# Attention scores of a fused fp32 block: two pairs of PSUM banks regrouped as three single banks, and a fourth bank for the row maxima

## What is computed

```python
q = (x @ wq).reshape(b, s, 32, 32)
k = (x @ wk).reshape(b, s, 8, 32);  v = (x @ wv).reshape(b, s, 8, 32)
k = jnp.repeat(k, 4, axis=2);       v = jnp.repeat(v, 4, axis=2)
scores = einsum('bihd,bjhd->bhij', q, k) * 32 ** -0.5
scores = where(causal, scores, finfo.min)
out = einsum('bhij,bjhd->bihd', softmax(scores), v).reshape(b, s, 1024)
x = layernorm(x + out @ wo)
```

## Time and profile before

| | us |
|---|---|
| median of 3 runs | 3541.24 |
| lowest, highest | 3540.5, 3547.18 |
| the profiled execution's own time | 3546.64 |
| its span, first to last instruction | 3544.9 |
| attention, in that span | 552.0 to 2607.6 |
| from one middle group's first exponential to the next one's | 125.5 |

### The profile page before, as it was taken

The page is one execution under the profiler, slowest core; times in us unless marked ns, Lnnn a source line. Parts: engine busy times, 40 slices in busy tenths (PEclk is TensorE's granted clock), DMA queues, the critical chain, the costliest instruction groups (busy, mean ns, idle before and its releaser), DMA issues. The chain is left out here.

```text
span 3544.9 us, 62208 instructions
## 1 busy us (share of the span) xinstructions
PE 3439.6 (97%) x25458; PEld 2429.2 (69%) x25458; DVE 1978.4 (56%) x3577; ACT 1468.0 (41%) x1839; POOL 1738.5 (49%) x747
## 2 busy tenths in 40 slices
PE   8999998999999999999999999999959999999999
PEld 7888885566666666666666666666538888888887
DVE  3122116777667677776767767776425666642222
ACT  3111112555555555555555555555532222221111
POOL 0000002888988898898889889889420000000000
PEclk9999997999999999999999999999979999999999
DMA  6344325121111111112111111210037778755553
GB/s 214 113 125 118 113 90 120 30 53 50 33 43 49 46 29 51 49 32 52 51 37 38 51 48 31 53 32 8 12 117 212 233 230 224 205 197 177 178 172 128
DMA packets 248221, 340.63 MB, mean 96 GB/s; under 512 B 55440, under 2 KB 150288, under 8 KB 247952
## 3 DMA queue, kind: packets, MB, share of 16 engines
q1 hardware_dynamic: 247952, 336.87, 32.3%
HBM read 203.08 MB, written 133.17 MB: 95 GB/s over the span
## 5 line engine op out<-in xcount | busy, mean ns | idle before, releaser
L683 DVE TENSOR_REDUCE p_part_max<-p_qm 128x1 f32<-128x512 f32 (+3 forms) x2240 | 1408.3, 671 | 578.3 <-PE p_qm L533 328.7
L503 POOL TENSOR_TENSOR p_psums<-p_psums,p_probs 128x1024 f32<-128x1024 f32 x620 | 1475.4, 2380 | 93.4 <-ACT p_probs L642 2.8
L646 ACT ACTIVATE p_probs<-p_km 128x1024 f32<-128x1024 f32 x896 | 878.8, 1021 | 480.7 <-PE p_km L561 411.1
L533 PE MATMUL p_qm<-p_k_st,p_q_st 96*128 96x512 f32 (+3 forms) x2560 | 913.5, 421 | 12.5 <-DMA p_q_st<-q_hi 10.8
L533 PEld LDWEIGHTS p_qm<-p_k_st,p_q_st 96*128 96x128 f32 x2560 | 481.1, 194 | 254.7 <-issue 113.0
L561 PE MATMUL p_km<-p_q_st,p_k_st 97*128 97x512 f32 x1792 | 599.5, 416 | 13.6 <-ACT p_probs L646 7.8
L568 PE MATMUL p_o<-p_probs,p_v 128*32 128x256 f32 (+1 forms) x9216 | 564.8, 371 | 0.0
L568 PEld LDWEIGHTS p_o<-p_probs,p_v 128*32 128x32 f32 x9216 | 270.7, 110 | 216.7 <-issue 45.1
L561 PEld LDWEIGHTS p_km<-p_q_st,p_k_st 97*128 97x128 f32 x1792 | 311.6, 191 | 112.9 <-ACT p_probs L646 73.5
L499 POOL TENSOR_TENSOR p_psums<-p_probs 128x1024 f32<-128x1024 f32 x110 | 261.7, 2379 | 222.1 <-ACT p_probs L646 222.1
L32 POOL MEMSET p_ident<- 128x128 f32 x2 | 0.4, 204 | 556.3 <-POOLq L63 543.5
(11 more groups left out here) (150 smaller groups left out, 4101.3 us busy)
## 6 DMA issues: line engine op xcount, KB each, us to landing
p_q_st<-q_hi SPq DMA_DIRECT2D x128, 256.0 KB, 4.7
p_x_raw<-in_xT SPq DMA_DIRECT2D x64, 256.0 KB, 3.5
q_hi<-p_out_hi SPq DMA_DIRECT2D x64, 256.0 KB, 2.0
q_lo<-p_out_lo SPq DMA_DIRECT2D x64, 256.0 KB, 2.3
p_q_st<-q_lo SPq DMA_DIRECT2D x64, 256.0 KB, 4.5
attended_T<-p_o_raw SPq DMA_DIRECT2D x128, 128.0 KB
p_a_raw<-attended_T SPq DMA_DIRECT2D x32, 512.0 KB, 4.8
p_recip<-reciprocals SPq DMA_DIRECT2D x128, 128.0 KB, 6.7
```

Source lines behind the costliest of these rows:

```text
L503: pool.tensor_tensor(sums[:, :, :], sums[:, :, :], probs[(n * NS + s) % PB][:, :, :], ALU.add).then_inc(added, 1)
L533: last = pe.matmul(bank[:, x * keys:(x + 1) * keys], q_st[par][0:ROWS, c, h + x, sub * P:(sub + 1) * P], k_st[par][0:ROWS, j * CK:j * CK + ...
L646: act.activation(tile[:, :, :].rearrange("p h q -> p (h q)"), km[s % 2][:, :, :].rearrange("p a b -> p (a b)"), ACT.Exp, scale=SCALE).then ...
L683: dve.reduce_max(part_max[c][:, h:h + heads, sub, j], qm[bank_of(i)][:, 0:item_width(i)].rearrange("p (h k) -> p h k", h=heads), AX.X).the ...
```

## The change

`QM` is 4. The scores have `KM` = 3 single banks instead of two pairs. A step is handled as a list of halves, `HALVES`: [0, 1] off the diagonal, [1, 0] in the first diagonal step, [1] in the second. Halves are counted through all groups, 136 in each. Each half is one bank, one count of `scored`, one activation of 512 elements and one count of `exp_done`; PE makes half u after exponential u - 3. Matmuls and their order are the same, and the banks in use stay 8: 4 + 3 + 1. All waits on `exp_done` and `scored` elsewhere are rewritten to the same points in counts of halves.

```diff
-    QM = 3
+    QM = 4
+    KM = 3
+    HALVES = [[1] if t == 2 * c + 1 else [1, 0] if t == 2 * c else [0, 1] for c, t in STEPS]
+    HALVES_BEFORE = [sum(map(len, HALVES[:s])) for s in range(NS + 1)]
+
+    def halves(n, s):
+
+        return n * HALVES_BEFORE[NS] + HALVES_BEFORE[s]
...
-        km = [ps(f"p2_km{i}", [P, 2, BANK]) for i in range(2)]
+        km = [ps(f"p2_km{i}", [P, BANK]) for i in range(KM)]
...
-                        sp.wait_ge(scored, n * NS + FIRST_STEP[2 * c + 2])
+                        sp.wait_ge(scored, halves(n, FIRST_STEP[2 * c + 2]))
...
-                        pool.wait_ge(exp_done, n * NS + s + 1)
+                        pool.wait_ge(exp_done, halves(n, s + 1))
...
             def scores(n, par, s):
                 c, t = STEPS[s]
-                at_least(pe, exp_done, n * NS + s - 1)
...
+                for i, x in enumerate(HALVES[s]):
+                    u = halves(n, s) + i
+                    at_least(pe, exp_done, u - KM + 1)
+                    if t >= 2 * c:
+                        four = km[u % KM][:, :].rearrange("p (h q) -> p h q", h=REP)
+                        masked = x == t - 2 * c
                         last = pe.matmul(four, keys, q_st[par][0:ROWS + 1, c // 2, :, q0 + x * P:q0 + (x + 1) * P],
-                                         start=True, stop=x > first)
...
+                                         start=True, stop=not masked)
+                        if masked:
+                            last = pe.matmul(four, ident_bf[:, :], mask_k[:, :].unsqueeze(1).to_broadcast([P, REP, P]),
+                                             start=False, stop=True)
+                    else:
+                        two = km[u % KM][:, :].rearrange("p (h q) -> p h q", h=2)
                         last = pe.matmul(two, keys, q_st[par][0:ROWS + 1, c // 2, 2 * x:2 * x + 2, q0:q0 + CQ],
                                          start=True, stop=True)
-                last.then_inc(scored, 1)
+                    last.then_inc(scored, 1)
...
-                pe.wait_ge(exp_done, n * NS + steps[-1] + 1)
+                pe.wait_ge(exp_done, halves(n, steps[-1] + 1))
...
-                act.wait_ge(scored, n * NS + s + 1)
...
+                for i, x in enumerate(HALVES[s]):
+                    u = halves(n, s) + i
+                    act.wait_ge(scored, u + 1)
+                    if t >= 2 * c:
+                        act.activation(tile[:, :, x * P:(x + 1) * P], km[u % KM][:, :].rearrange("p (h q) -> p h q", h=REP),
+                                       ACT.Exp, scale=SCALE).then_inc(exp_done, 1)
+                    else:
+                        act.activation(tile[:, 2 * x:2 * x + 2, :].rearrange("p h q -> p (h q)"), km[u % KM][:, :],
+                                       ACT.Exp, scale=SCALE).then_inc(exp_done, 1)
```

More of the change, by code:

```diff
@@ L439, in group @@
                     if what == "load q":
-                        sp.wait_ge(scored, n * NS + FIRST_STEP[2 * c + 2])
+                        sp.wait_ge(scored, halves(n, FIRST_STEP[2 * c + 2]))
                         load_q(b2, g2, par, c)
                     elif what == "load k":
-                        sp.wait_ge(scored, n * NS + FIRST_STEP[NC - 1] + SUB * (c + 1))
+                        sp.wait_ge(scored, halves(n, FIRST_STEP[NC - 1] + SUB * (c + 1)))
                         load_k(b2, g2, par, c)
@@ L545, in scores @@
                 c, t = STEPS[s]
-                at_least(pe, exp_done, n * NS + s - 1)
                 if t == 0 and c % 2 == 0:
                     pe.wait_ge(m_in[par][c // 2], q_loads(n, par) // 3)
[L549 to L553, removed]
-                        last = pe.matmul(four, keys, q_st[par][0:ROWS + 1, c // 2, :, q0 + x * P:q0 + (x + 1) * P],
-                                         start=True, stop=x > first)
[L556 to L560, removed]
+                keys, q0 = k_st[par][0:ROWS + 1, t * P:(t + 1) * P], (c % 2) * CQ
+                for i, x in enumerate(HALVES[s]):
[4 more added lines that the diff above has]
+                        masked = x == t - 2 * c
+                        last = pe.matmul(four, keys, q_st[par][0:ROWS + 1, c // 2, :, q0 + x * P:q0 + (x + 1) * P],
+                                         start=True, stop=not masked)
[4 more added lines that the diff above has]
+                        two = km[u % KM][:, :].rearrange("p (h q) -> p h q", h=2)
                         last = pe.matmul(two, keys, q_st[par][0:ROWS + 1, c // 2, 2 * x:2 * x + 2, q0:q0 + CQ],
                                          start=True, stop=True)
-                last.then_inc(scored, 1)
+                    last.then_inc(scored, 1)
             def weighted(lhs, rhs, at, o, first):
```

## The result

The changed kernel takes 3568.8 us (median of 4 runs, 3565.0 to 3572.8) against 3544.1 before, a ratio of 1.007 with a 95% interval of 1.0054 to 1.0085. Timed again beside other kernels it gave 3567.3 against 3543.7, 1.0071 (1.0051 to 1.009). So it is slower by 24 to 25 us where 15 were forecast. The measured 3568.8 lies inside the stated range, 3532 to 3584, and 12 us over its likeliest value, 3557.

The account below looks back on a forecast made before the run. The prediction took PE's stream plus PE's waits as the bound. Middle groups +20 us, opening -7.4 and closing +2.8 summed to +15 us, 3557 us against the median of the runs, range 3532 to 3584.

Parts of the forecast that it names:

- What bounds: Attention's middle groups: no other engine is full, so a group costs PE's stream issue time plus PE's waits.
- Score banks: Score steps: a second half newly waits for the step just before; slot loss 0.41 to 0.46 us, group score waits 6.4.
- Cadence of exponentials: ACT's queued halves start 0.495 us apart, so a split step costs ACT 0.99 us where it cost 0.92.
- The fourth maxima bank: Maxima tiles: one more bank removes nearly all of the 1.9 us a group PE waits for DVE.
- The middle groups: The 14 like attention groups: both parts together +1.4 us a group, +20 us in 14.
- The granted clock: PE's clock in the 14 groups: stays at 1.00 with twice as many score waits, 0 us.
- The opening: Opening attention group, bound by DVE: the fourth bank gives 8.7 us, both parts together give 7.4 back.
- Signs: Right: groups near 127 us, opening some 6 us shorter; wrong: group under 125 us, maxima waits remaining, clock under 1.00.
- The split costs more: Rival: halves 0.52 apart or starts 0.54 after their matmul, ACT bounding the slot; 3565 to 3575, 0.25 of slower's 0.73.
- The parts cancel: Rival: queued halves at 0.46 to 0.48, or a dearer maxima wait; within 7 us, 3541, chance 0.17.
- the fourth bank does nothing: Rival: PE now arrives late at the maxima banks anyway; +22 to +55 us, no separate chance given.
- the free split: Rival: splitting exponentials is free and only the fourth maxima bank shows, -33 us, 3508; chance 0.10.

Follow-up runs that it names:

- experiment 1: Changed kernel with four single score banks and three maxima banks in place of three and four: 3513.4 us, 0.9912 of the kernel before.
- experiment 4: Changed kernel with one maxima tile moved in between the two halves of a step: 3505.7 us, 0.9887 of the kernel before.
- experiment 3: Kernel before, its pairs of banks kept, with each 1024-element exponential made as two of 512 and one count a step: 3559.9 us, 1.0041.
- experiment 2: Changed kernel with three maxima banks in place of four, three score banks kept, one bank unused: 3622.4 us, 1.0213 of the kernel before.
- experiment 8: Changed kernel with a maxima tile between the halves and the second group's loads issued after the first group's second row maximum: 3498.0 us, 0.9873.
- experiment 5: Changed kernel run again unaltered for a second profile: 3567.3 us, 1.0071 of the kernel before.
- experiment 6: Changed kernel with the second group's k, q and v loads issued after the first group's second row maximum: 3560.8 us, 1.0044.
- experiment 9: Kernel before with two maxima banks in place of three: 3726.9 us, 1.0509.
- experiment 7: Changed kernel with four score banks, three maxima banks and a maxima tile between the halves: 3493.8 us, 0.9856 of the kernel before.

## Why the prediction was right, and where it was short

*What bounds.* Right. A group is PE's stream plus PE's waits.

*Score banks.* The step held in every number of the slot, and the waits came to 5.9 us a group for a forecast 6.4. The new wait is that of the second half for the exponential of the half three back. Experiment 1 gives it its bank back and all of the loss goes; experiment 4 puts work into the wait and most of it goes.

*Cadence of exponentials.* 0.495 was taken, 0.493 measured with eight on end. Experiment 3, which is this term by itself, came to 15.4 us for an expected 10 to 18; but its middle groups gave 0.9 us each for 1.2, and the two more dips of its closing group made up for that, so the agreement of the whole is in part luck. The start of an exponential after its matmul was taken as 0.51 and is 0.52.

The Trainium skill (ScalarE: Activation LUTs, "What ACT_TABLE_LOAD costs") has a fixed 186 ns in each activation and 93 ns of overlap on end, by which a split step costs 93 ns more. Here two halves on end take 2 x 0.493 = 0.99 us where a whole one took 0.91 to 0.92, so 0.07 more: the rows were the better price.

*The fourth maxima bank.* Worth 2.4 us a group under split scores by experiment 2, where the prediction's terms give 2.3 (maxima waits 2.8 to 0, score waits 5.9 to 6.4). Maxima waits of 1.0 us a group remained, where none were forecast.

*The middle groups.* 126.7 against 125.5 is +1.2 a group where +1.4 was forecast; over 14 groups 17 us for 20. The rest of the 23.8 measured is the clock.

*The granted clock.* This step failed: "I leave it there with twice as many, 0". Four dips of 3.4 us in the middle groups cost 6.6 us. In the closing group there are four against one before. The closing groups of experiments 4 and 8, with the same banks and order inside the group, differ by two dips and 3.4 us, and those of the changed kernel, experiment 5 and experiment 6, with four, three and two dips, take 135.1, 133.5 and 131.7 us: 1.7 us a dip. So the three more cost 5.1. These 12 us are more than the distance from 15 to 25. In the closing group, +7.0 for a forecast +2.8, the rest after the dips is +1.9.

*The opening.* 7.4 us were to come back, 3.8 came. The reckoning had PE, DVE and ACT in it but left out the transfer of the row maximum: "all transfers stay" is true of the list, not of when they are asked for. PE came earlier, the transfer queue did not. Experiment 6 shows it: 6.5 us on the kernel. It shows too that 7.4 was no right price for the rest: with the late loads the opening, from its first maxima tile, takes 160.5 us, 10.4 under the kernel before. The prediction had no term for the clock in the opening, while it rose 26 us earlier in the changed kernel; what the bank and the clock are each worth there, no run here separates. So the 3.8 hides two misses of opposite sign.

Together: 17.2 (middle) + 11.7 (clock) - 3.8 (opening) + 1.9 (closing) = 27 us for attention, whose stretch grew by 26.9. The middle groups without dips and the closing one came out 4 us under the forecast together, the opening 4 us over it. That these offset each other is luck, and the clock is what is left.

*Signs.* Of the prediction's own signs of being right, the 2176 exponentials of 0.597 us, the groups near 127 us and the waits of a slot's second step are there; the waits were 35 a group, most of them short, and the opening was 3.8 us shorter, not 6. Of its signs of being wrong two are there in part: maxima waits remained, and the clock was under 1.00 inside four groups.

*Rivals.* "The split costs more" named 3565 to 3575, where the measured time lies, but its conditions (halves 0.52 apart, or starts at 0.54) did not come: 0.493 and 0.52. That its number fits is chance. "The parts cancel" and "the fourth bank does nothing" fell, the latter by experiment 2. As to the free split: splitting is not free where it costs a bank; where it does not (experiment 1) it is worth 31 us. The rule that was set beside this rival (the Trainium skill, Perfetto Trace Analysis, "Optimizing Scalar/DVE Operations": unsaturated Scalar that causes bubbles, so break up instructions) thus held with four score banks, 0.9912, and not with three, 1.007, unless other work stood between the halves (experiment 4, 0.9887). What decides is how many halves PE may be ahead, and what it has to do before it needs the next bank.

*Open.* What brings the dips. In middle groups they were in the kernels with three score banks and both halves on end (changed, experiments 2, 5 and 6), nine of them with the longer waits of experiment 2, and every one began 63.5 to 65.2 us after its group's first exponential, behind PE's wait of 1.13 us for the last row maximum. But that wait is as long before the change and in experiments 1, 3 and 9, which have no dips there, so it isn't enough by itself; experiment 4, with the same banks in another order, has it at 0.8 us and has none either. Closing groups had dips in most kernels, and none in experiments 1, 7 and 8. No run here tells the cause.

## What to carry to other kernels

Smaller pieces helped here only where each was released by itself (not in experiment 3) and as many buffers stayed in flight as before, or other work stood between the pieces: two pairs let PE run four banks ahead of ACT, three singles only three. Where a producer must wait for a piece, try another stream's work between the pieces before dealing out banks; here it was worth 63 us with the same instructions. A stage that gets faster asks for its inputs earlier, so look at what is queued ahead of the small transfer that it will wait for.

## What was not expected of the hardware

Stretches of 3.4 us at the lower level of TensorE's clock inside a stage in which PE is 98% busy, three or four in 1780 us, all at the same place of a group and two of them in the same groups in two executions (1034 and 1543 us of either span). Ten or eleven groups of the fourteen, with the same instructions and waits, had none. Each cost its group about half its length, 1.5 to 1.8 us. And an 8 KB transfer that took 13.5 us to land behind 25 larger ones of the same queue, against 1.8 for most of its kind.
